# A graph network's edge stream: a block's counts leave PSUM in three casts of 1024, 512 and 1024 columns, with three signals each way

## The reference, cut to what matters

```python
# layer 1: a message for every edge, summed by target node, then a GRU cell
h = relu(concat([x[src], edge_attr]) @ W1.T + b1)
agg = segment_sum(h @ W2.T + b2, dst)
gi, gh = agg @ Wih.T + bih, x @ Whh.T + bhh
r, z = sigmoid(i_r + h_r), sigmoid(i_z + h_z);  n = tanh(i_n + r * h_n)
x = layernorm(x + (1 - z) * n + z * x)
# layer 2: the mean of the sources' rows by target node
mean = segment_sum(x[dst], src) / maximum(deg, 1)
x = layernorm(x + mean @ weight + x @ root_weight + bias)
```

## Time and profile before

| what | us |
|---|---|
| median of 3 runs | 4222.97 |
| the three runs | 4222.5, 4222.97, 4232.51 |
| the profiled execution: its own time | 4234.13 |
| the profiled execution: its span | 4232.7 |
| mean granted TensorE clock | 0.93 |
| PE, DVE, ACT, POOL busy | 3850.8, 2821.0, 2350.7, 3047.4 |

### The profile page before, as it was taken

The page is one execution under the profiler, slowest core; times in us unless marked ns, Lnnn a source line. Parts: engine busy times, 40 slices in busy tenths (PEclk is TensorE's granted clock), DMA queues, the critical chain, the costliest instruction groups (busy, mean ns, idle before and its releaser), DMA issues.

```text
span 4232.7 us, 87235 instructions
## 1 busy us (share of the span) xinstructions
PE 3850.8 (91%) x30236; PEld 3421.7 (81%) x30236; DVE 2821.0 (67%) x7211; ACT 2350.7 (56%) x4230; POOL 3047.4 (72%) x3223
## 2 busy tenths in 40 slices
PE   5688999998999998999999999999998999999986
PEld 4667888797979787978888888879797979787875
DVE  4676667666666666666666666766666666666547
ACT  2476555556555555555555556555655555555414
POOL 2677777777777777777777777777777777777731
PEclk8798999999999898999999999999999999899999
DMA  7744657575757565666666565757575756566556
GB/s 204 147 142 133 174 148 181 147 182 141 187 142 183 146 177 149 173 159 166 162 162 167 154 174 147 182 144 183 144 185 143 184 145 178 149 172 156 156 138 158
DMA packets 1016895, 683.91 MB, mean 162 GB/s; under 512 B 818071, under 2 KB 857316, under 8 KB 1016073
## 3 DMA queue, kind: packets, MB, share of 16 engines
q1 hardware_dynamic: 828003, 292.94, 29.6%
q0 software_dynamic: 104320, 217.85, 19.5%
q10 hardware_dynamic: 84134, 167.43, 12.4%
HBM read 497.94 MB, written 179.87 MB: 160 GB/s over the span
## 4 chain that ended last, share of the span: by engine, by line
PE 32%; POOL 31%; issue 13%; DVE 8%; DMA 7%; ACT 3%; DVEq 0%; SPq 0%; POOLq 0%; ACTq 0%
POOL ring L903 25%; PE stream_psw L1397 9%; PE stream_pse L1374 7%; PE stream_pse L1382 7%; PE stream_psa L1391 6%; POOL stream_yg L903 6%; DMA ring<-y,ring 5%; DVE stream_col L1109 2%; ACT stream_a_sb L1002 2%; DMA stream_yg<-y,ring 1%; ACT stream_hid L933 1%; DVE ring L1087 1%; DVE stream_row L1104 1%; PE stream_psw L1434 1%; DVE stream_twin L1092 1%
## 5 line engine op out<-in xcount | busy, mean ns | idle before, releaser
L903 POOL DMA_INDIRECT ring<-y,ring x2495 | 2376.8, 953 | 768.5 <-issue 711.3
L1002 ACT CAST stream_a_sb<-stream_psa 98x512 fp8e3<-98x512 f32 x3125 | 1756.4, 586 | 1128.3 <-PE stream_psa L1391 1070.5
L1391 PE MATMUL stream_psa<-stream_col,stream_row 128*98 128x256 f16 x6250 | 1174.3, 288 | 194.2 <-ACT stream_a_sb L1002 148.0
L1397 PE MATMUL stream_psw<-stream_strip,stream_z 128*128 128x256 fp8e3 x9130 | 1297.1, 274 | 21.6 <-DVE stream_sums L1119 18.1
L1087 DVE TENSOR_TENSOR ring<-stream_pse,ring 128x384 f32<-128x384 f32 x1000 | 486.1, 486 | 967.6 <-DMA ring<-y,ring 810.0
L1382 PE MATMUL stream_pse<-w1b,ring 128*128 128x128 f32 x6250 | 1028.8, 299 | 62.5 <-DVE ring L1087 38.3
L1109 DVE TENSOR_TENSOR stream_col<-stream_psa,stream_twin 128x1536 f16<-128x1536 f16 x1250 | 1016.6, 815 | 0.0
L1391 PEld LDWEIGHTS stream_psa<-stream_col,stream_row 128*98 128x98 f16 x6250 | 734.8, 131 | 323.8 <-ACT stream_a_sb L1002 227.7
L1397 PEld LDWEIGHTS stream_psw<-stream_strip,stream_z 128*128 128x128 f16 x9130 | 891.0, 98 | 123.2 <-issue 31.7
L1382 PEld LDWEIGHTS stream_pse<-w1b,ring 128*128 128x128 f32 x6250 | 873.2, 206 | 108.9 <-issue 66.1
L1374 PEld LDWEIGHTS stream_pse<-stream_seg,stream_hid 128*128 128x128 f32 x6250 | 794.2, 202 | 1.4 <-ACT stream_hid L933 0.8
(11 more groups left out here) (205 smaller groups left out, 1594.9 us busy)
## 6 DMA issues: line engine op xcount, KB each, us to landing
A<-stream_a_sb ACTq DMA_DIRECT2D x625, 245.0 KB
stream_strip<-A SPq DMA_DIRECT2D x1862, 80.0 KB
ring<-in_ea_blocks_dram SPq DMA_DIRECT2D x625, 160.0 KB
ring<-y,ring POOLq DMA_INDIRECT x2500
stream_yg<-y,ring POOLq DMA_INDIRECT x625
prologue_xt<-in_xT_dram SPq DMA_DIRECT2D x14, 448.0 KB, 5.8
y<-prologue_ysb SPq DMA_DIRECT2D x14, 448.0 KB, 4.5
out_dram<-stream_hid ACTq DMA_DIRECT2D x24, 256.0 KB, 3.7
```

The source lines that it names most:

```text
L903: nc.gpsimd.indirect_dma_start(out=yg[s.c % YR][:, t, :], out_offset=None, in_=h.y, in_offset=bass.IndirectOffsetOnAxis(ap=idx[s.c // (PH ...
L1002: nc.scalar.copy(a_sb[n % AR][0:RW, j, :], psa[BANK[j]][0:RW, :], saturate=False).then_inc(a_out, 1)
L1391: last = nc.tensor.matmul(psa[BANK[j]][0:RW, e * LOS:(e + 1) * LOS], row1[s.c % 2][:, 2 * j + e, :], col1[s.c % 2][:, 2 * j + e, :], start ...
L1397: last = nc.tensor.matmul(bank[:, 0:LOS], zz[:, n // 2, n % 2, :], tiles[:, n // 2, :], start=(first and n == 0), stop=(final and n == hi ...
```

## The change

ACT casts a block's counts in three instructions: pairs 0 and 1 together (1024 columns, banks 0 and 1), pair 2 alone (512 columns, bank 2), pairs 3 and 4 together (1024 columns, banks 0 and 1). PE signals `a_done` after pairs 1, 2 and 4 only, and ACT signals `a_out` three times a block. `SPENT` becomes (0, 0, -1, 1, 1) in units of three: pairs 0 and 1 both need the whole block before cast, pair 2 its first two casts, pairs 3 and 4 both need the first cast of their own block. The store of the block before and the early gate work stand behind the first cast (before: behind cast 1), and Relu behind the second, which is pair 2 (before: behind cast 3).

```diff
-SPENT = [max(x - PAIRS if x >= j else x for x in range(PAIRS) if BANK[x] == BANK[j]) + 1 for j in range(PAIRS)]
+PARTS = ((0, 2), (2, 3), (3, 5))
+SPENT = (0, 0, -1, 1, 1)
...
             def store_a(s):
-                act.wait_ge(a_out, s.times(PAIRS, PAIRS))
+                act.wait_ge(a_out, s.times(len(PARTS), len(PARTS)))
...
-                    for j in range(PAIRS):
-                        act.wait_ge(a_done, a.times(PAIRS, j + 1))
-                        nc.scalar.copy(a_sb[n % AR][0:RW, j, :], psa[BANK[j]][0:RW, :], saturate=False).then_inc(a_out, 1)
-                        if j == 1 and n >= 1:
+                    for part, (lo, hi) in enumerate(PARTS):
+                        act.wait_ge(a_done, a.times(len(PARTS), part + 1))
+                        nc.scalar.copy(a_sb[n % AR][0:RW, lo:hi, :].rearrange("p g l -> p (g l)"),
+                                       psa4[0:RW, 512 * BANK[lo]:512 * BANK[lo] + 512 * (hi - lo)], saturate=False).then_inc(a_out, 1)
+                        if part == 0 and n >= 1:
                             store_a(a.back(1))
-                        if j == 1 and k is not None:
+                        if part == 0 and k is not None:
                             early_gate_work(k, ph)
-                        if j == 3 and n == counted(s.c)[0]:
+                        if part == 1 and n == counted(s.c)[0]:
                             relu(s)
...
-                reach(dve, a_done, s.times(PAIRS, -PAIRS))
+                reach(dve, a_done, s.times(len(PARTS), -len(PARTS)))
...
-                reach(pe, a_out, s.times(PAIRS, SPENT[j]))
+                reach(pe, a_out, s.times(len(PARTS), SPENT[j]))
...
-                last.then_inc(a_done, 1)
+                if j + 1 in (hi for _, hi in PARTS):
+                    last.then_inc(a_done, 1)
...
-                        pe.wait_ge(a_out, BLOCKS * PAIRS)
+                        pe.wait_ge(a_out, BLOCKS * len(PARTS))
```

## The result

| | before | after |
|---|---|---|
| median, us | 4227.74 (4 runs, 4222.5 to 4233.01) | 4259.05 (4 runs, 4239.7 to 4269.87) |
| ratio | | 1.0073, 95% interval 1.0055 to 1.009 |
| span of the profiled execution | 4232.7 | 4238.3 |
| clock, mean | 0.93 | 0.932 |

The forecast was 4223 us and a range up to 4236. The 5.6 us hide a larger loss in the stream: the last gather starts at 4084.60 us, 11.2 us later than before, and the closing part behind it happened to be shorter (153.7 us against 159.3; over all thirteen profiles it lies between 151.3 and 161.7, with no relation to the casts).

A forecast was written before the change was run, and what follows sets the result against it. POOL's gathers were taken to bound the kernel; all cast, signal and Relu terms came to 0 on the end, so the median of the runs, 4222.97 + 0, gave 4223 us, with a range of 4217 to 4236.

The forecast's parts named there:

- What bounds the kernel: Whole stream: POOL is an unbroken queue of 3120 gathers at 1.26 us each, with under 4 us of real waiting for PE.
- Casts and Relu one cast earlier: ACT: a 1024-column cast takes 1.00 us, saving 0.34 us a block but nothing in time; earlier Relu isn't needed by POOL.
- The blocks with units: Pair 0 there starts 1.03 us later, paid once; loop 5.71 us, TensorE 6.06 us, both under POOL's 6.25; margin 0.19 us.
- TensorE's waits for `stream_a_sb`: Sign of being right: these waits rise from 148.0 us, nearly once a block, at pair 0.
- DVE's waits for gathers: Sign of being right: DVE's waiting for gathers to land stays at about 800 us, as before.
- in most blocks: Sign of being wrong: DVE's second add waits for PE in most blocks.
- Blocks with two blocks' counts: 13 double blocks, blocks 8 to 32: each 0.4 to 0.9 us behind, at most 12 us; taken as 0, up to 3.
- The time regained: Double blocks end 0.4 us behind DVE; the ordinary block between two of them can make up 6.25 - 5.71 = 0.5 us.
- The clock: Double blocks: 2.9 us of PE work twice as long at the lower clock; up to 3 us if it falls on most.
- Rival 2: Blocks with units: short TensorE standstills lower its clock, 6 us lost in each of 18 phases, 4331 us; chance 0.02.
- The room: Mid-stream: PE, DVE and ACT may fall 19.9 us, three blocks, further behind before POOL loses anything.
- Rival 1: Waits at pair 0 add up in blocks with units: 7 us lost in each of 18 phases, 4349 us; chance 0.03.

The follow-up runs named there:

- x4: Changed kernel with five 512-column casts instead of the long ones, signals kept after the second, third and fifth, Relu behind the third: 4250.51 us, 1.0067 of before.
- x5: Kernel before with only Relu moved, behind the third of its five casts, five signals kept: 4218.95 us, 0.9997 of before.
- x7: Changed kernel plus idle matmuls on PE in blocks 8 to 33, where it would wait: 4230.86 us, 1.0021 of before.
- x1: Changed kernel run once more without an edit, against before: 4244.86 us, 1.0052 of before.
- x2: Changed kernel, but with five casts, five signals and the old place of Relu up to block 34: 4221.92 us, 1.0004 of before.
- x6: Changed kernel with Relu behind the third cast (pairs 3 and 4) instead of the second: 4214.1 us, 0.9989 of before.
- x11: The kernel of x6 unchanged, measured again with more rounds: 4223.15 us, 0.9991 of before.
- x8: Against before: pairs 3 and 4 in one cast, pairs 0, 1 and 2 in one each, Relu behind pair 2: 4239.42 us, 1.0048 of before.

## Why the prediction was wrong

**What bounds the kernel: right.** POOL, with gathers 1.25 us apart, before and after. The loss that the profiles show in the stream is POOL standing still: over the whole stream 20.3 us of waiting for PE beyond the 0.3 us, against 3.7 before.

**Casts and Relu one cast earlier: right.** The long cast takes 1008 ns; x4 shows that the longer instruction is not what costs, and x5 that the place of Relu costs nothing with five casts. That two signals fewer are worth nothing by themselves was not tested apart from the later release that they bring.

**The blocks with units: right, for a block.** This was called the place that the change had to be judged by. In after, PE before pair 0 of two blocks in a row:

```profile
2140.71 0.39 PE L1393 MATMUL stream_psa<-stream_col,stream_row 128*98 128x256 f16 x2 [0.52 <-ACT stream_a_sb L1003]
...
2146.91 0.39 PE L1393 MATMUL stream_psa<-stream_col,stream_row 128*98 128x256 f16 x2
```

It stands still once, 0.52 us, and the blocks are 6.20 us apart. The clock there kept its upper level (2.4 GHz), as in the window of 129 us that answers to the third of the earlier trace rows:

```profile
2080.00:2209.00 129.00, 125.77 (x1114) 117.25 (x1112) 89.12 (x216) 66.82 (x84) 97.62 (x104) 1.00 0.69 178
```

Two signs were off. TensorE's waits for `stream_a_sb` were to come nearly once a block; they rose from 148.0 to 259.1 us, but in 208 places, as many as before. And DVE's waits for gathers were to stay near 800 us (810.0 in the earlier trace rows), and fell to

```profile
DVE ring L1089 <- DMA ring<-y,ring: 462.6, 284, 4.1
DVE ring L1089 <- PE stream_pse L1384: 358.3, 367, 5.9
```

so DVE now waits for PE in a good part of the blocks: 468 times over all five buffers, against 146 before. The prediction had named such waits "in most blocks" as a sign of being wrong. The consumers are later than they were, and in mid-stream POOL had room for it.

**"Blocks with two blocks' counts": the step that failed**, in three terms.

1. *The time regained.* The loop was given as 4.92 + 2.9 us to the end of `edge_product`, which makes about 8.3 us to the next Relu; measured with the upper clock 8.51 (among others, 0.05 us was taken for the signal from the cast to PE, and 0.15 us lies between the two in after). That size was nearly right. But the double block was called 0.4 us late against a block of before that itself took 7.87 us (Relu at 239.78 to 247.65), and the 0.5 us that the ordinary block was to make up came from the 5.71 us of a block *with units*. The loop over both is 8.51 + 4.66 = 13.2 us, and POOL has 12.5 us for both. Nothing is made up; a pair loses 0.7 us. At the upper clock the change makes the pair 2.2 us longer (13.2 for 11.0), and 1.5 us of that was in hand. I had set each half against its own due time and never added up the loop over the two.
2. *The clock.* Named ("twice as long at the lower clock") and then taken as up to 3 us in all. It costs 1.0 us a pair (after against x7), more than the 0.7 us by which the loop is over POOL's time. Rival 2 had the right mechanism and the wrong place: in the blocks with units TensorE stays busy 97% of the time; in the double blocks it has nothing else to do while it waits.
3. *The room.* 19.9 us was read from Relu to the gather that reuses its buffer. POOL's second wait, for `edge_product` of the block four before, binds earlier; it stands in POOL's four lines of code, and in the earlier trace rows as the releaser PE with 2.8 us. By it the room in mid-stream is 16.4 us (the matmuls of the block that ends at 2123.2 on POOL are done at 2125.9, and the gather that needs them starts at 2142.2). And it was needed at 190 us, just behind the start, where it is far smaller. POOL's first long wait of after (251.55) is in front of block 17 and so for block 13, the end of the third pair. Those three pairs, from the Relu of block 8 at

```profile
212.17 0.74 ACT L934 ACTIVATE stream_hid<-ring 128x640 f32<-128x640 f32 x1 [0.69 <-DVE ring L1089]
```

to that of block 14 at 255.96, took 43.8 us, 6.3 more than 30 gathers; 1.5 us of it POOL stood. There was room for some 5 us, a quarter of the figure used. The change had itself taken part of it: before, the Relu of block 8 is at 205.63, 6.5 us earlier. It is 2 us earlier already at the first Relus of the stream, and the rest comes of the ordinary blocks ahead of block 8, whose steps grow from 4.2 to 4.67 us.

All thirteen pairs end with the Relu of block 34:

```profile
398.52 0.74 ACT L934 ACTIVATE stream_hid<-stream_yg 128x640 f32<-128x640 f32 x1 [0.69 <-DVE stream_yg L1089]
```

That is 186.4 us for 162.5 us of gathers: 23.9 us over, less 5 us of room, is 19 us; the profiles show 19.5 and 20.9. In x7, 13 pairs x 0.7 = 9 us, less 5, is 4; its profile shows 4.0. So with the right room, the loop alone would have cost 4 us, and the other 15 us are the clock. How much the ordinary blocks ahead of the first double block add was not tested apart.

**The rest of the time.** 20 us are 0.47%. Runs of before and after differ by 0.52% in the second comparison, which fits, and by 0.73% in the first, whose interval (from 1.0055) lies above it. In its four runs the time rises as the mean clock falls (0.932 at 4239.7 us, 0.931, 0.929, 0.928 at 4269.87), so more of the lower clock may be the reason. None of the three longer runs has a profile, the five runs of x1 show such an order only loosely (0.938 at 4237.0 us, 0.933 at 4249.6), and this stays open.

**Rival 1** was the mechanism: standstills at pair 0 in a loop through Relu, the long cast and `segment` that exceeds POOL's time. It had a chance of 0.03, because it was priced in the phases, where x2 shows that it costs nothing.

The Trainium skill's rule ("TensorE: Matmul & The Clock Gate", section "A second HAM failure mode: psum-queue depth-cycling"), that small idles between matmul groups cycling through PSUM banks make the clock swing, fits what the double blocks of after show: a clock of 1.00 in the short step and 0.81 or 0.64 in the long one, where PE waits for banks, and 1.00 in both in x7, with matmuls in the waits. Whether only waits between banks do this, or any standing still of PE, no run here tells apart.

## What to carry to other kernels

When a producer (here POOL) is the bound and its consumers have room, judge a longer dependency where the room is smallest and the consumers' own work thinnest, not where the busiest engine is fullest, and add the loop up over the whole repeating pattern. Joining casts lets go of a bank later; put no other instruction between the last matmul and the cast that frees its bank: in x6 and x11, with Relu behind the last cast instead of in front of it, the same three casts were level with the kernel before. Read all waits of the producer before its room is taken from one of them.

## What the runs showed of the hardware

TensorE's clock made more of the loss than the waits that went with it: 28 matmuls a pair of blocks that compute nothing, placed in the waits, raised the granted clock from 0.84 to 0.98 and took the standstill of POOL from 20 to 4 us, and the time from 1.0052 to 1.0021 of before. In x8, one long cast a block, behind Relu, went with a clock of 0.81 over the same stretch and cost nearly as much as the whole change (1.0048 of before against 1.0052).
